# A decoder layer on one core: seven block products for eight in its FFN, and the last normalisation on ScalarE

## The reference

```python
x = _layernorm(x + _L0_attn_ref(x, L0_attn_w_qkv, L0_attn_w_o), axis=-1)
x = _layernorm(x + _L0_xattn_ref(x, ctx_4096, L0_xattn_Wq, L0_xattn_bq, L0_xattn_Wk, L0_xattn_bk), axis=-1)
x = _layernorm(x + _L0_ffn_ref(x, L0_ffn_qweight, L0_ffn_lut4, L0_ffn_lut8, L0_ffn_bias), axis=-1)
```

```python
w_l = dequant_kbit(qweight, lut4, B_L)
y_l = jnp.einsum('bsi,oi->bso', x, w_l)
y = jnp.where(mask[..., None], y_h, y_l) + bias
```

## Time and profile before

| | us |
|---|---|
| median of 3 runs (1274.96 to 1282.88) | 1276.9 |
| the profiled execution | 1276.45 |
| its span, first to last instruction | 1274.7 |
| TensorE busy (8230 matmuls) | 1250.8 |
| VectorE busy | 876.3 |
| ScalarE busy | 530.4 |
| GpSimd busy | 524.8 |

### The profile page before, as it was taken

One profiled execution on the slowest core, in us unless ns is written; L12 is line 12 of the kernel. 1 busy time (PEld: TensorE's weight loads), 2 busy tenths in 40 slices (PEclk: granted clock), 3 DMA queues, 4 the chain that ended last, 5 costly groups with the idle time before them and its releaser, 6 DMA issues.

```text
span 1274.7 us, 25314 instructions
## 1 busy us (share of the span) xinstructions
PE 1250.8 (98%) x8230; PEld 1057.4 (83%) x8230; DVE 876.3 (69%) x2491; ACT 530.4 (42%) x1597; POOL 524.8 (41%) x448
## 2 busy tenths in 40 slices
PE   8999999999999999999999999999999999999997
PEld 6888889998778888888877887888888888888886
DVE  7999999566778878878866974353543536566564
ACT  4131203456777787787750223342523433110110
POOL 3512122368666776776740000535433450222221
PEclk9999999998999999999999999999999999999999
DMA  8165436573964444444441224024152419222221
GB/s 283 69 215 169 159 110 218 152 206 110 218 193 126 124 143 125 125 138 130 125 159 64 69 67 167 16 96 169 66 199 66 178 32 352 99 81 84 99 92 57
DMA packets 135450, 170.43 MB, mean 134 GB/s; under 512 B 36688, under 2 KB 100176, under 8 KB 134736
## 3 DMA queue, kind: packets, MB, share of 16 engines
q1 hardware_dynamic: 135376, 169.47, 41.7%
HBM read 112.80 MB, written 56.62 MB: 133 GB/s over the span
## 4 chain that ended last, share of the span: by engine, by line
PE 74%; issue 12%; DVE 5%; POOL 4%; DMA 2%; SPq 2%; ACT 1%; POOLq 0%; DVEq 0%; ACTq 0%
PE bank L872 13%; PE bank L681 12%; PE bank L683 12%; PE bank L682 12%; PE bank L809 6%; PE bank L794 5%; PE bank L767 5%; POOL x2b L2005 3%; PE bank L837 3%; PE bank L732 2%; PE bank L991 1%; PE bank L841 1%; DVE bits L1491 1%; PE bank L763 1%; DMA vv<-v_scr 1%
## 5 line engine op out<-in xcount | busy, mean ns | idle before, releaser
L1915 POOL TENSOR_TENSOR prob<-prob,rinv 128x512 f32<-128x512 f32 x192 | 206.7, 1078 | 150.3 <-DVE rinv L1580 150.2
L1196 ACT ACTIVATE prob<-bank,nmax 128x256 f32<-128x256 f32 (+1 forms) x512 | 212.1, 431 | 77.9 <-DVE nmax L1572 71.7
L1572 DVE CUSTOM_DVE_ANT_0 bank<-bank,mask 128x256 f32<-128x256 f32 (+1 forms) x512 | 170.1, 385 | 36.6 <-PE bank L794 26.3
L809 PE MATMUL bank<-ident,prob 128*128 128x128 f32 x768 | 115.9, 274 | 2.2 <-POOL prob L1915 1.5
L809 PEld LDWEIGHTS bank<-ident,prob 128*128 128x128 f32 x768 | 94.9, 141 | 26.4 <-POOL prob L1915 3.3
L1196 ACT ACTIVATION_READ_ACCUMULATOR prob<-bank,nmax 128x1 f32 x512 | 109.8, 215 | 0.0
L872 PE MATMUL bank<-wo_hi,att_hi 128*128 128x512 f32 x256 | 104.5, 408 | 2.6 <-issue 2.6
L794 PE MATMUL bank<-k,q 96*128 96x256 f32 (+1 forms) x512 | 104.4, 306 | 2.2 <-DMA vv<-v_scr 2.2
L1731 DVE SCALAR_TENSOR_TENSOR k_lo<-bank,bA,k_hi 128x512 fp32r<-128x512 f32 x32 | 24.0, 752 | 115.2 <-ACT k_hi L1329 114.7
L681 PE MATMUL bank<-f_hi,x2T_hi 128*128 128x512 f32 x256 | 101.0, 395 | 0.8 <-DVE x2T_lo L1427 0.8
L872 PE MATMUL bank<-wo_lo,att_hi 128*128 128x512 f32 x256 | 101.6, 397 | 0.0
(11 more groups left out here) (203 smaller groups left out, 3167.3 us busy)
## 6 DMA issues: line engine op xcount, KB each, us to landing
q<-qk_scr SPq DMA_DIRECT2D x192, 128.0 KB, 2.4
x_st<-x_scr SPq DMA_DIRECT2D x32, 512.0 KB, 3.9
qk_scr<-rot SPq DMA_DIRECT2D x60, 256.0 KB, 2.6
xc_in<-x_cols SPq DMA_DIRECT2D x32, 256.0 KB, 4.8
y<-x SPq DMA_DIRECT2D x16, 512.0 KB, 3.5
x_scr<-y SPq DMA_DIRECT2D x16, 512.0 KB, 2.7
cx_in<-ctx_in SPq DMA_DIRECT2D x16, 512.0 KB, 4.8
x_scr<-x_st SPq DMA_DIRECT2D x16, 512.0 KB, 3.2
```

The costliest lines, as they stand in the source:

```text
L809: mm = nc.tensor.transpose(tb[:, at * P:(at + 1) * P], prob[:, k % 4, c:c + P], ident[:, :])
L1196: mm = nc.scalar.activation(prob[:, k % 4, i * keys:(i + 1) * keys], SBANK[pos][:, i * keys:(i + 1) * keys], ACT.Exp, bias=nmax[:, k % 4, ...
L1572: mm = nc.vector.tensor_tensor_reduce(part, part, mask[:, 2 * P - keys:2 * P], 1.0, BIGGEST, ALU.add, ALU.min, nmax[:, k % 4, i:i + 1])
L1915: nc.gpsimd.tensor_tensor(pr, pr, rinv[:, k % 4, 0:n].unsqueeze(2).to_broadcast([P, n, keys]), ALU.mult)\
```

## The change

The FFN works on pairs of tiles. With the pair's tokens as two rows of blocks and the 1024 input features as two columns, A is 2 x 2 blocks (A11, A12, A21, A22), F is 2 x 2 blocks of 512 x 512, and Winograd's form of Strassen's algorithm makes the four output blocks of seven products instead of eight. VectorE makes four sums of A blocks for each pair (`sums`: S1 to S4; A21 alone is first copied out of PSUM by ScalarE), GpSimd their low parts (`sum_low`). Four sums of F blocks (T1 to T4) are made once, by GpSimd in `weight_sums`, on slices of 256 rows that SP brings in and out during stage 4 (`load_window`, `store_window`, tile win, which lies on d_hi, d_lo and cu). F is stored whole and not split (one plane; `f_low` is gone, `f_high` copies in float32), and split in the last group and the first pair of the FFN: `f_unit_high` on ScalarE, `f_unit_low` on GpSimd for B11, B21, T2, T1 and T4, on VectorE for T3 and B22.

Three of the products' sums stay in one bank (U): it is read by VectorE after each product, and the next product adds to it. So TensorE waits within a pair for VectorE's additions (`y3_part`). The additions go straight into the residual's tile, to which GpSimd has added the bias (`add_bias`). GpSimd makes a scale and a shift (`rstd3`), and ScalarE normalises (`normalise3`). The rows of x2 are in a ring of six tiles. In stage 4 `key_sum` and `key_diagonals` come one key block later, and stages 4 and 5 of SP, and stage 5 of all engines, are written out instead of looped.

```diff
+            def sums(q):
...
+                t11, t12, t22 = X2PS[0][:, :], X2PS[1][:, :], X2PS[3][:, :]
...
+                nc.vector.tensor_tensor(s1, x2_a21[:, :], t22, ALU.add).then_inc(sum_step, 1)
+                nc.vector.tensor_tensor(s3, t11, x2_a21[:, :], ALU.subtract).then_inc(sum_step, 1)
+                dve.wait_ge(sum_step, 4 * q + 1)
+                nc.vector.tensor_tensor(s2, s1, t11, ALU.subtract).then_inc(sum_step, 1)
+                dve.wait_ge(sum_step, 4 * q + 3)
+                nc.vector.tensor_tensor(s4, t12, s2, ALU.subtract).then_inc(sum_step, 1)
...
                 for it in range(1, KT):
                     key_low(g, a, it)
-                    if 2 <= it < 2 + GT:
-                        key_sum(g, it - 2)
+                    if 3 <= it < 3 + GT:
+                        key_sum(g, it - 3)
                     if it == 5:
                         x1_low(g, 0)
-                    if it == 6:
+                    if it == KT - 1:
                         key_diagonals(g)
```

TensorE, one pair (`part_product` is 4 x 3 matmuls, high x high, high x low, low x high):

```diff
+            for q in range(TWOS):
+                u, base = U_BANK[q % 2][:, :], PARTS * q
+                pe.wait_ge(x2T_lo_ready, 3 * q + 1)
...
+                part_product(q, A11, u, True, False)
...
+                part_product(q, A12, P2_BANK[:, :], True, True)
+                if q + 1 < TWOS:
+                    wait(pe, sum_step, 4 * q + 4)
+                    turn_x2(2 * q + 2)
+                pe.wait_ge(sum_lo_ready, 4 * q + 1)
+                pe.wait_ge(y3_part, base + U1_OUT)
+                part_product(q, S2, u, False, False)
+                if q + 1 < TWOS:
+                    pe.wait_ge(x2T_lo_ready, 3 * q + 3)
+                    turn_x2(2 * q + 3)
+                pe.wait_ge(sum_lo_ready, 4 * q + 2)
...
+                part_product(q, S1, P5_BANK[:, :], True, False)
+                pe.wait_ge(sum_lo_ready, 4 * q + 3)
+                pe.wait_ge(y3_part, base + U2_OUT)
+                part_product(q, S3, u, False, False)
+                pe.wait_ge(sum_lo_ready, 4 * q + 4)
+                pe.wait_ge(y3_part, base + P5_OUT)
+                part_product(q, S4, P5_BANK[:, :], False, True)
+                pe.wait_ge(x2T_lo_ready, 3 * q + 3)
+                pe.wait_ge(y3_part, base + U3_OUT)
+                part_product(q, A22, u, False, True)
```

VectorE, one pair:

```diff
+            part_low(0, A11)
+            part_low(0, A12)
+            sums(0)
+            add_last(GROUPS - 1, 1, GT - 1)
+            for q in range(TWOS):
...
+                if q == 0:
+                    stats_last(GROUPS - 1, GT - 1)
+                part_low(q, A22)
+                dve.wait_ge(x2b_ready, 2 * q + 1)
+                add_part(q, U1_OUT, A11, u, 0, 0)
...
+                add_part(q, C11_OUT, A12, P2_BANK, 0, 0)
+                half_stats(q, C11_OUT, 0, 0)
+                if q == 0:
+                    f_unit_low(F_T3)
+                add_part(q, U2_OUT, S2, u, 0, 1)
+                if q + 1 < TWOS:
+                    part_low(q + 1, A11)
+                    part_low(q + 1, A12)
+                if q == 0:
+                    f_unit_low(F_B22)
...
+                add_part(q, P5_OUT, S1, P5_BANK, 1, 1)
+                if q + 1 < TWOS:
+                    sums(q + 1)
...
+                add_part(q, U3_OUT, S3, u, 1, 1)
+                half_stats(q, U3_OUT, 1, 1)
+                add_part(q, C12_OUT, S4, P5_BANK, 0, 1)
...
```

ScalarE:

```diff
+            for q in range(1, TWOS):
+                part_high(q, A11)
+                part_high(q, A12)
+                a21_out(q)
+                for i in (S2, S1, S3, S4):
+                    part_high(q, i)
+                normalise3(2 * q - 2)
+                part_high(q, A22)
+                normalise3(2 * q - 1)
```

GpSimd:

```diff
+            add_bias(0)
+            f_unit_low(F_T1, (0,))
+            sum_low(0, S2)
+            f_unit_low(F_T1, (1,))
+            rstd2(GROUPS - 1, GT - 1)
+            sum_low(0, S1)
+            add_bias(1)
+            sum_low(0, S3)
+            sum_low(0, S4)
+            f_unit_low(F_T4)
+            for q in range(TWOS):
+                if q:
+                    rstd3(2 * q - 1)
+                if q + 1 < TWOS:
+                    add_bias(2 * q + 2)
+                    add_bias(2 * q + 3)
+                    for i in (S2, S1, S3):
+                        sum_low(q + 1, i)
+                rstd3(2 * q)
+                if q + 1 < TWOS:
+                    sum_low(q + 1, S4)
```

More of the change, by code:

```diff
@@ L57 @@
 IN_ROT = PAIRS * FULL + 4
+HALF = KT // 2
+PARTS = 7
+TWOS = TILES // 2
+RING = 6
 EARLY = 5
@@ L640, in stage4_group @@
+            sp.wait_ge(f_stored, 16 * BATCH)
+            load_window(0)
+            store_window(0)
+            def stage4_group(g):
+                sp.wait_ge(acc_done, use_of(g, key_use(KT - 1)) + 1)
+                load_cols(g + 1, cT_in)
                 for t in range(GT):
-                    if t == GT - 1 and not last:
+                    if t == GT - 1:
                         sp.wait_ge(acc_done, use_of(g, att_use(GT - 1, 1, False)) + 1)
                         load_ctx(g + 1)
+                        store_window(g + 1)
@@ L644, in stage4_group @@
                     store_x2(g, t)
-                    if last and t == 1:
-                        sp.wait_ge(s2_done, GT * GROUPS)
-                        sp.dma_start(bias_bc[:, :], bias.rearrange("(a n) -> a n", a=1).to_broadcast([P, D])).then_inc(bias_ld, 16)
-                    if t and not last:
-                        load_x1(g + 1, t - 1)
-                if not last:
-                    load_x1(g + 1, GT - 1)
-            with sp.Fori(0, GROUPS - 1) as g:
-                stage4_group(g, False)
@@ L677, in _ @@
+            for j in range(2):
+                sp.wait_ge(out_stored[j], 16 * TWOS)
         @block.tensor
@@ L1096, in _ @@
             cross_group(GROUPS - 1, 1, True)
-            pe.wait_ge(f_ld, 32 * KT)
-            def ffn_batch(b, last):
-                for j in range(2):
-                    n = 2 * b + j
-                    pe.wait_ge(x2T_lo_ready, n + 1)
-                    for half in range(2):
-                        wait(pe, y3_part, 2 * n - 2)
-                        for kt in range(KT):
-                            mm = product(YPS[j][half][:, :], x2T_hi[:, j, kt, :], x2T_lo[:, j, kt, :],
-                                         f_hi[:, kt, half * BANK:(half + 1) * BANK],
-                                         f_lo[:, kt, half * BANK:(half + 1) * BANK], kt == 0, kt == KT - 1)
-                        mm.then_inc(ffn_done, 1)
-                        if half == 0 and not (last and j == 1):
-                            pe.wait_ge(x2_ld[1 - j], 16 * b + 16 * (j + 1))
-                            turn(x2_st[:, 1 - j, :], X2PS, x2ps_ready)
@@ L1115, in _, with part_product @@
-            ffn_batch(0, False)
-            with pe.Fori(1, BATCH - 1) as b:
-                ffn_batch(b, False)
-            ffn_batch(BATCH - 1, True)
+            def part_product(q, i, o, first, last):
+                for kt in range(HALF):
+                    if q == 0 and kt % 2 == 0 and i in BY_POOL:
+                        pe.wait_ge(f_lo_ready, BY_POOL[i] + kt // 2 + 1)
+                    if q == 0 and kt == 0 and i in BY_DVE:
+                        pe.wait_ge(f_lo2_ready, BY_DVE[i] + 1)
+                    a_hi, a_lo = (w[:, i, kt * P:(kt + 1) * P] for w in (x2T_hi, x2T_lo))
+                    b_hi, b_lo = f_hi[i][:, kt, :], f_lo[i][:, kt, :]
+                    nc.tensor.matmul(o, a_hi, b_hi, start=first and kt == 0, stop=False, skip_group_check=True)
+                    nc.tensor.matmul(o, a_hi, b_lo, start=False, stop=False, skip_group_check=True)
+                    mm = nc.tensor.matmul(o, a_lo, b_hi, start=False, stop=last and kt == HALF - 1, skip_group_check=True)
+                mm.then_inc(ffn_done, 1)
@@ L1859, in _, with add_part, half_stats @@
-            ffn_batch(0, False)
-            with dve.Fori(1, BATCH - 1) as b:
-                ffn_batch(b, False)
-            ffn_batch(BATCH - 1, True)
+            def add_part(q, step, part, source, j, half):
+                y = x2_slot(2 * q + j)[:, half * BANK:(half + 1) * BANK]
+                dve.wait_ge(ffn_done, PARTS * q + part + 1)
+                nc.vector.tensor_tensor(y, source[:, :], y, ALU.add).then_inc(y3_part, 1)
+            def half_stats(q, step, j, half):
+                dve.wait_ge(y3_part, PARTS * q + step)
+                nc.vector.bn_stats(st3[:, j, half, :], x2_slot(2 * q + j)[:, half * BANK:(half + 1) * BANK]).then_inc(y3_stats, 1)
@@ new lines, in cross_group, with f_unit_low @@
+                    if last and t in F_LOWS_AT:
+                        f_unit_low(F_LOWS_AT[t])
+                    if last and t == GT - 1:
+                        return
+                    rstd2(g, t)
+            F_LOWS_AT = {0: F_B11, 1: F_B21, 2: F_T2}
+            def f_unit_low(i, halves=(0, 1)):
+                for h in halves:
```

(4 more changed lines are left out.)

397 lines of the change are left out of this document (272 added, 125 removed).

## The result

The changed kernel takes 1262.88 us (median of four runs, 1260.07 to 1264.91) against 1275.93 for the kernel before: 0.990 of its time, 95% interval 0.9875 to 0.9919, so 13.05 us or 1.0% less. The forecast was 1267, range 1259 to 1272; its narrower own range, 1265 to 1269.5, did not hold.

What follows compares the result with a forecast made beforehand. TensorE was taken to bound the FFN (busy 187.70 of 188 us). Products -21.7, join -2.4, diagonals +1.4, stalls +9.8, clock +2.7, end +0.8 sum to -9.4: 1276.45 to 1267 us, range 1259 to 1272.

Steps and rivals of the forecast that it cites:

- The products: FFN matmuls fall from 768 to 672 of the same shape, 0.2264 us each: -21.7 us.
- The join: Between cross-attention and FFN, TensorE's two idle gaps (1.36 and 0.78 us) go: -2.4 us.
- The diagonals: In the cross-attention groups, key_diagonals one step later delays a matmul by 0.36 us in each of four groups: +1.4 us.
- The end: After the last product, a second small GpSimd operation and ScalarE's 1.24 us replace VectorE's 0.81: +0.8 us.
- Pairs from the third on: FFN pairs after the first two: no stall counted, 20.86 us of TensorE work per pair.
- The exclusion: VectorE's T3 and B22 low parts (two SBUF inputs) and GpSimd wait for each other: 4.6 us added to GpSimd's row.
- The stalls of the first two pairs: TensorE waits in the FFN's first two pairs for GpSimd's almost unbroken row of work: +9.8 us together.
- the chain named for S2 of pair 1: Before the second pair's S2: GpSimd's pow, ScalarE's normalise3(0), A22's high part, VectorE's low part and U1 addition; 3.4 us.
- the three signs of being wrong: TensorE at pair 1's S2 by 1112, pairs 2 to 7 over 21.5 us, or earlier groups growing by over 1 us.
- the clock, +2.7: Half clock for about six us, paid once after the roughly 5 us wait before S2 of pair 1: +2.7 us.
- I watched T1: Late-loads rival: T1, expected near 1076.6, comes 4 us late and moves GpSimd's row by 4: 1271 us, chance 0.11.
- the one without a clock loss, 1264.3: Rival: the array is not throttled after the longer wait before S2, so 2.7 us less: 1264.3 us, chance 0.15.

Runs made afterwards that it cites:

- the other execution: The kernel after, unchanged, measured and profiled once more against the kernel before: 1262.18 us, ratio 0.9902.

## Why the prediction came out as it did

**Right, by its own steps.** The products: 672 matmuls, pairs 2 to 7 at 20.84 us against 20.86, the -21.7 whole. The join: no idle, -1.7 there and -0.92 in the FFN for the transposes that moved, -2.6 against -2.4. The diagonals: 0.33 per group against 0.36. The end: +0.75 against +0.8. Pairs from the third on: no stall. The exclusion: GpSimd held for 3.7 us, and 3 to 4 us by experiment, against 4.6. The stalls of the first two pairs: 8.3 against 9.8, with the chain named for S2 of pair 1 as it ran. S2 of pair 1 began 35.5 us behind the FFN's first matmul, against a forecast of 37.05 (1116.1 - 1079.05); 0.9 of the 1.5 between them is that the two low parts held GpSimd for 3.7 us and not for their whole 4.6. None of the three signs of being wrong came (S2 at 1112.66, pairs of 20.84, groups 0.33 longer).

**Wrong: the clock, +2.7.** I took it as one sure loss behind one wait of about 5 us. There was no such wait in the profiled execution, and the loss was 0. In other executions of this FFN the half clock took away 1.7 us, which cost the FFN nothing (173.15 us, ahead of S2 of pair 1), or 3.4, which cost it 2.9 (176.02, behind it). So the term is no sure price, and it depends on where the loss falls.

**Wrong: how the stalls fall.** I put half of them before S2 of pair 1. The row loads of tile 2 (1.41 us, 2.51 in the other execution) were no term at all: I watched T1, and T1 came in time. And B22's low part, which I had only counted as time taken from GpSimd, held VectorE's own next addition: that is the 3.37 us before S4. The sum survived because S2 of pair 1 starts when GpSimd's row lets it, 35.5 us in, in four profiles with four different splits. That two misjudged waits left the total alone is the strength of that term and not of my reading of them.

With the terms as measured: -21.7 (products) - 2.6 (join) + 1.7 (diagonals 1.3, and the unexplained gap of 0.4) + 8.3 (stalls) + 0 (clock) + 0.75 (end) + 0.3 (outside the span) = -13.3. The medians say -13.05. My -9.4 missed by the clock (2.7) and by 1.5 of the stalls, about 4 us. Of the rivals the one without a clock loss, 1264.3, was nearest, though for another reason than it gave: the long wait itself was missing.

## What to carry to other kernels

When a stage's tiling changes, the steady state is the easy term, and it came out to the tenth of a us in each pair. What is lost sits in the first iteration, where weights, rows and splits that used to be spread are wanted at once: write out each engine's row there, and look for the instruction that is queued behind a wait on its own engine (`normalise3` ahead of a high part, B22 ahead of an addition). Reordering four queues there gave some 5 us more (1257.3 against 1262.2 and 1262.9), over a third of what the change itself had brought. Moving the row loads alone brought nothing: a weight then came late, and ScalarE's and VectorE's queues stood behind it.

## What the runs showed of the hardware

In these runs the length of a wait doesn't say whether the clock falls, nor for how long. Waits of over 1.3 us in the FFN and the loss in the same stretch, worked out as (1 - granted clock) x its length:

| wait, us | clock lost, us |
|---|---|
| 1.34 to 1.83 (fifteen waits) | 0 |
| 1.97 | some 1.7 |
| 2.15, 2.38 | 0 |
| 2.51 | 1.7 |
| 2.54 | 0 |
| 3.12 | 1.7 |
| 3.37, 3.38 | 0 |
| 3.37 | 1.7 |
| 3.34, 3.40 | some 3.4 |
| 4.02, 6.81 | 3.4 |

The level is always 0.50 (1.2 GHz), and the loss comes in two sizes, 1.7 and 3.4 us, that is 3.4 or 6.8 us at 0.50; about the same 1.8 and 3.3 stand behind the 2.55 us wait that every execution has. The 3.4 are not all paid: with 3.34, 3.40, 4.02 and 6.81 the clock fell some 1.0 to 2.6 us before the wait was over. And the 1.7 us behind `u_bc` came with no such wait at all. The Trainium skill, "TensorE: Matmul & The Clock Gate", section "HAM oscillation — how this bites in real kernels", tells of one loss per long gap; here it was one for 4.02 and 6.81, and from 1.97 to 3.40 some had it and some had not, with nothing in these traces that says which.
